# Experts' token lists made inside the experts' stage, in column strips, and causal masks over two tiles

## The reference, cut to what matters

```
# causal layer: 12 heads of width 16, T = 256
att = einsum('bhqd,bhkd->bhqk', q, k) * D ** -0.5
att = where(tril(ones((T, T))), att, -inf)
# experts: n = 8192 tokens, E = 16, capacity = 1024
scores = sigmoid(x @ gate_weight.T)
topk_score, topk_ids = top_k(scores.T, capacity)      # per expert, over the tokens
xg = x[topk_ids]
out = (silu(xg @ Wg) * (xg @ Wu)) @ Wd * topk_score
y = zeros((n, d)).at[topk_ids].add(out)
```

## Time and profile before

| | us |
|---|---|
| median of 3 runs | 5709.36 |
| lowest and highest run | 5707.49, 5717.35 |
| profiled execution, its own time | 5669.09 |
| its span in the profile | 5667.3 |
| TensorE busy in the span | 5117.5 (90%) |
| VectorE busy | 3504.7 (62%) |
| ScalarE busy | 2573.6 (45%) |
| GpSimd busy | 1120.5 (20%) |

### The profile page before, as it was taken

One profiled execution on the slowest core, in us unless ns is written; L12 is line 12 of the kernel. 1 busy time (PEld: TensorE's weight loads), 2 busy tenths in 40 slices (PEclk: granted clock), 3 DMA queues, 4 the chain that ended last, 5 costly groups with the idle time before them and its releaser, 6 DMA issues. The chain is left out here.

```text
span 5667.3 us, 119255 instructions
## 1 busy us (share of the span) xinstructions
PE 5117.5 (90%) x41810; PEld 4014.3 (71%) x41810; DVE 3504.7 (62%) x8939; ACT 2573.6 (45%) x5128; POOL 1120.5 (20%) x1056
## 2 busy tenths in 40 slices
PE   0799999999999999999999999699999822899999
PEld 0578777777778777778777777477777612677777
DVE  6566666666666666666666666577777577222222
ACT  0355555555555555555555555355555500111111
POOL 6111111111111111111111111000000002333343
PEclk9999999999999999999999999899999956999999
DMA  6544444444444444444444444244444200333332
GB/s 104 102 96 93 86 98 94 103 94 95 86 96 96 103 92 95 87 94 97 103 94 95 87 96 95 68 90 92 95 96 92 70 6 6 98 65 82 85 86 40
DMA packets 1283993, 488.96 MB, mean 86 GB/s; under 512 B 1086531, under 2 KB 1270560, under 8 KB 1283872
## 3 DMA queue, kind: packets, MB, share of 16 engines
q1 hardware_dynamic: 1256224, 450.68, 36.5%
q0 software_dynamic: 27648, 36.72, 4.1%
HBM read 162.87 MB, written 60.28 MB: 39 GB/s over the span
## 5 line engine op out<-in xcount | busy, mean ns | idle before, releaser
L754 ACT ACTIVATE pT<-banks 128x384 f32<-128x384 f32 x1920 | 924.9, 491 | 785.4 <-PE banks L524 785.0
L972 DVE TENSOR_REDUCE mx<-banks 128x4 f32<-128x768 f32 x768 | 719.0, 949 | 293.6 <-PE banks L506 293.5
L1155 POOL TENSOR_TENSOR rstd<-ve,half 128x2 f32<-128x2 f32 x288 | 218.8, 760 | 3069.5 <-DVE ve L881 3069.5
L504 PE MATMUL banks<-maskb,eyeb 128*128 128x384 bf16 x1920 | 633.8, 330 | 52.2 <-DMA qkT<-stack 25.3
L506 PE MATMUL banks<-qkT 128*128 128x192 bf16 (+2 forms) x3840 | 634.6, 247 | 0.0
L524 PE MATMUL banks<-qkT 128*128 128x192 bf16 (+2 forms) x3840 | 632.3, 247 | 0.0
L622 PE MATMUL banks<-w,pT 128*128 128x192 f32 x3072 | 554.5, 330 | 0.0
L622 PEld LDWEIGHTS banks<-w,pT 128*128 128x128 f32 x3072 | 492.7, 190 | 42.4 <-issue 21.9
L522 PE MATMUL banks<-mseq,eyeb 128*128 128x384 bf16 x1536 | 501.4, 326 | 10.0 <-DMA qkT<-mrT 5.7
L608 PE MATMUL banks<-nT,w 128*128 128x256 f32 x1920 | 473.3, 383 | 7.2 <-DMA b<-in_b 3.1
L1915 PE MATMUL ps_g<-exp_xT,exp_wg 64*128 64x512 f32 x1152 | 476.0, 594 | 1.0 <-ACT exp_xT L1829 1.0
(11 more groups left out here) (202 smaller groups left out, 8909.9 us busy)
## 6 DMA issues: line engine op xcount, KB each, us to landing
hcur<-hbuf SPq DMA_DIRECT2D x164, 192.0 KB, 2.6
resid<-hbuf SPq DMA_DIRECT2D x160, 192.0 KB, 2.5
amb<-am_d SPq DMA_DIRECT2D x130, 192.0 KB, 3.0
hbuf<-hout SPq DMA_DIRECT2D x128, 192.0 KB, 2.0
exp_wg<-in_ewg SPq DMA_DIRECT2D x16, 768.0 KB
exp_wu<-in_ewu SPq DMA_DIRECT2D x16, 768.0 KB
exp_wd<-in_ewd SPq DMA_DIRECT2D x16, 576.0 KB
xs<-xr SPq DMA_DIRECT2D x32, 272.0 KB, 2.2
```

The source lines that it names most:

```text
L504: nc.tensor.matmul(dst[:, 0:SCOLS], eyeb[:], maskb[:, masks, :], start=True, stop=False)
L754: ph.inc(nc.scalar.activation(pT[s][:, h % NPT, :], bank[s][h % 2][:, 0:SCOLS], ACT.Exp, scale=SCALE), "p", s)
L972: last = nc.vector.tensor_reduce(mx[s][:, :, at].rearrange("p t h -> p h t"), src[:, :, 0:SCOLS].rearrange("p h (t k) -> p h t k", t=T), A ...
```

## The change

`choose` and `experts` become one block, `route`. All weights' loads of the first two experts are issued at its start, behind the inputs of the search. The search, the ranks and the transposes are as before. GpSimd makes no table steps any more; all four are VectorE's. Lists 0 and 1 and the table of list 2 come before the loop; list j of the others is made two experts ahead, inside the loop: its products between `gate_up` and `transposes`, its table's four steps one behind each quarter of `weigh` of the expert before. The 64 products of a list go in turn to four column strips (16 to each), so that the result is four partial lists on 128 partitions; VectorE joins place and group (`read_strips`), a product with a 0/1 matrix adds the four strips (`ids_sum`), VectorE reads the list (`read_ids`), SyncE stores it and loads it back. The list's results share the banks of `ps_y`, so `down` waits until the list is read. In the causal layer the mask product covers the two diagonal tiles only, 256 columns in place of 384, and the other tile starts from what the score product writes.

```diff
+        def pe_mask(ph, dst, mask):
+            part = lambda x: x[:, 0:SCOLS]
+            if ph is not tok:
+                part = lambda x: x[:, 0:SCOLS].rearrange("p (x c) -> p x c", c=P)[:, 0:3:2, :]
+            nc.tensor.matmul(part(dst), eyeb[:], part(mask), start=True, stop=ph is not tok)
...
-            nc.tensor.matmul(dst[:, 0:SCOLS], eyeb[:], maskb[:, masks, :], start=True, stop=False)
+            pe_mask(ph, dst, maskb[:, masks, :])
...
+            def keep_ids(j, u):
+                sp.wait_ge(idi_ok[u], j + 2)
+                dst = ids_d[bass.ds(j * 2 + u, 1), :].rearrange("o (h l) -> (o h) l", l=32)
+                sp.dma_start(dst, ids_i[u][:]).then_inc(ids_st[u], 16)
+
+            def load_ids(j, u):
+                sp.wait_ge(ids_st[u], j * 16 + 17)
+                sp.dma_start(idx[u][:], ids_d[bass.ds(j * 2 + u, 1), :].rearrange("o (p g) -> (o p) g", g=G)
+                             ).then_inc(i_in[u], 16)
             for u in U:
-                load(u, u)
+                weights(u, u)
+            for u in U:
+                keep_ids(0, u)
+                load_ids(0, u)
             with sp.Fori(0, E // 2 - 1) as i:
                 for u in U:
+                    keep_ids(i + 1, u)
                     sp.wait_ge(y_st, (i * 2 + u + 1) * (16 * G))
-                    load(i * 2 + u + 2, u)
+                    load_ids(i + 1, u)
+                    weights(i * 2 + u + 2, u)
...
+            def table_step(j, u, k):
+                grid = [P, NBLK, SEG, 32]
+                lane = iotab[:].unsqueeze(1).unsqueeze(1).to_broadcast(grid)
+                part = lambda w: hlT[:, w, :, bass.ds((j * 2 + u) * SEG, SEG)].unsqueeze(3).to_broadcast(grid)
+                if k == 0:
+                    dve.wait_ge(idp_ok[u], j + 1)
+                    lo = oh_lo[u][:].rearrange("p (c s) w l -> p c s w l", s=SEG)
+                    nc.vector.tensor_tensor(lo[:, :, :, 0, :], lane, part(1), ALU.is_equal).then_inc(oc[u], 1)
...
+            def read_strips(j, u):
+                dve.wait_ge(idp_ok[u], j + 2)
+                nc.vector.tensor_copy(ids_f[u][:], ps_id[u][:, 0:32]).then_inc(if_ok[u], 1)
+                dve.wait_ge(if_ok[u], j + 1)
+                nc.vector.scalar_tensor_tensor(out=ids_s[u][:], in0=ps_id[u][:, 32:64], scalar=float(P),
+                                               in1=ids_f[u][:], op0=ALU.mult, op1=ALU.add).then_inc(strip_ok[u], 1)
+
+            def read_ids(j, u):
+                dve.wait_ge(sum_ok[u], j + 1)
+                dve.wait_ge(ids_st[u], j * 16 + 1)
+                nc.vector.tensor_copy(ids_i[u][:], ps_sum[u]).then_inc(idi_ok[u], 1)
...
+                    hidden(i * 2 + u)
+                    read_strips(i + 1, u)
+                    read_xT(i * 2 + (u + 1), (i + 1, u))
+                    weigh(i * 2 + u, u, i + (1 + u) if u < tables else None)
...
+            def ids(j, u):
+                pe.wait_ge(y_ok, (j * 2 + (u - 2)) * NX + 1 if not isinstance(j, int) or j else 1)
+                pe.wait_ge(oh_ok[u], j + 1)
+                pe.wait_ge(hi_ok[u], j + 1)
+                pe.wait_ge(idi_ok[u], j + 1)
+                for t in range(NTILE):
+                    n = t % 4
+                    last = nc.tensor.matmul(ps_id[u][32 * n:32 * n + 32, :], oh_hi[u][:, t, :],
+                                            oh_lo[u][:, t].rearrange("p w l -> p (w l)"),
+                                            start=(t < 4), stop=(t >= NTILE - 4), tile_position=(0, 32 * n))
+                last.then_inc(idp_ok[u], 1)
+
+            def ids_sum(j, u):
+                pe.wait_ge(strip_ok[u], j + 1)
+                nc.tensor.matmul(ps_sum[u], strip[:], ids_s[u][:], start=True, stop=True).then_inc(sum_ok[u], 1)
...
+                if listed:
+                    pe.wait_ge(idi_ok[u], i + 3)
                 pe.wait_ge(hid_ok, e * NF + (NF + 1))
...
                 gate_up(i, 0)
-                transposes(i, 1)
+                ids(i + 1, 0)
+                transposes(i, 1, (i + 1, 0))
                 down(i, 0)
```

More of the change, by code:

```diff
@@ L204, in build @@
         tower(nc, a, hbuf, am_d, xs, sd, out, B, L)
-        choose(nc, a, sd, ids_d, N, CAP)
-        experts(nc, a, xs, ids_d, out, N, CAP)
+        route(nc, a, xs, sd, ids_d, out, N, CAP)
 def embed(nc, a, hbuf, am_d, B, V, HROWS):
@@ L1530, in choose @@
     NTILE = SEG * NBLK
-    HI = CAP // 32
+    G = CAP // P
+    HALF = 512
+    NHALF = CAP // HALF
+    y_out = out.rearrange("b s d -> (b s) d")
+    U = (0, 1)
     with ExitStack() as ctx:
-        sb = lambda name, shape, dt: ctx.enter_context(nc.sbuf_tensor("sel_" + name, shape, dt))
         sem = Semaphores(nc)
[L1535 to L1565, removed]
@@ new lines, in _, with gather, scatter @@
+            sp.wait_ge(y_st, 16 * G * E)
+        @block.gpsimd
+        def _(pool):
+            def gather(i, u):
+                wait_apart(pool, i_in[u], i * 16 + 16, eye_in, 16)
+                for g in range(G):
+                    pool.indirect_dma_start(xg[u][:, g, :], None, xs,
+                                            bass.IndirectOffsetOnAxis(ap=idx[u][:, g:g + 1], axis=0)
+                                            ).then_inc(g_in[u], 16)
+            def scatter(i, u):
+                if not (isinstance(i, int) and i * 2 + u == 0):
+                    pool.wait_ge(y_st, (i * 2 + u) * (16 * G))
+                for g in range(G):
+                    if g % 2 == 0:
+                        wait_apart(pool, y_ok, (i * 2 + u) * NX + (g // 2 + 2), eye_in, 16)
+                    pool.indirect_dma_start(y_out, bass.IndirectOffsetOnAxis(ap=idx[u][:, g:g + 1], axis=0),
+                                            yb[u][:, g, :], None, compute_op=ALU.add).then_inc(y_st, 16)
+            pool.wait_ge(eye_in, 16)
+            gather(0, 0)
+            gather(0, 1)
+            for u in U:
+                scatter(0, u)
+                gather(1, u)
+            with pool.Fori(1, E // 2 - 1) as i:
+                for u in U:
+                    scatter(i, u)
+                    gather(i + 1, u)
+            for u in U:
+                scatter(E // 2 - 1, u)
@@ L1698, in _ @@
+            for k in range(4):
+                table_step(1, 0, k)
+                if k == 1:
+                    read_strips(0, 1)
+                if k == 3:
+                    read_ids(0, 1)
+            read_xT(0)
+            with dve.Fori(0, E // 2 - 2) as i:
+                pair(i, 2)
+            pair(E // 2 - 2, 1)
+            hidden(E - 2)
+            read_xT(E - 1)
+            weigh(E - 2, 0)
+            hidden(E - 1)
+            weigh(E - 1, 1)
         @block.tensor
@@ L1887, in transposes @@
+            def transposes(i, u, listed=None):
                 e = i * 2 + u
@@ L1889, in transposes @@
                 for k in range(NX):
+                    if k == 2 and listed is not None:
+                        ids_sum(*listed)
                     if k >= 2:
```

349 lines of the change are left out of this document (147 added, 202 removed).

## The result

| | before, us | changed, us |
|---|---|---|
| median | 5708.42 (4 runs, 5701.23 to 5717.35) | 5543.12 (4 runs, 5541.42 to 5553.33) |
| profiled execution, its own time | 5669.1 | 5544.2 |
| its span | 5667.3 | 5542.4 |

The account below looks back on a forecast made before the run. TensorE was taken to bound the causal layer and experts, with VectorE's list making between them. -149 + 29 - 17 = -137 us from a median of 5709.4 gave 5573 us; 8-in-10 range 5530 to 5609.

Parts of the forecast that it names:

- Front, -149: From the first table step to an expert's first transposes: making only the first lists ahead saves 149 us, bounds 144 to 152.
- The hold-up of the first gather: Before the experts: VectorE, still making list 2's table, can hold up GpSimd's gathers; +2 us taken.
- Lists inside the experts, +29: In the experts: 14 lists' products on TensorE at 2.1 us each add 29 us, bounds +10 and +44.
- GpSimd's hold-up: In each expert: VectorE's four table steps may hold the scatter up by at most 7.6 us, hidden by the gathers' room.
- Masks, -17: Causal layer: mask products over two tiles save 0.54 us a turn over 31 full turns, 17 us; bounds 0 and -41.
- The offset of 40.3 us: Whole kernel: the median before lies 40.3 us above the profiled execution, and the change was taken to leave that untouched.
- masks in full: Rival, causal layer: the shorter masks pay all 41 us, giving 5548 us; chance 0.10.
- masks for nothing: Rival, causal layer: the shorter masks pay nothing, giving 5590 us; chance 0.12.
- the list's chain as a wait: Rival, experts: reading strips, sum and list takes twice 1.7 us, down products start 0.9 us late, +13 us, 5586; chance 0.06.
- GpSimd beyond its room: Rival, experts: GpSimd is held up some 15 us instead of 7.6, costing 3 us x 14, 5615 us; chance 0.07.
- the emptied array: Rival, list products: each change of strip empties TensorE's array, 14.5 us a list, 5746 us, slower; chance 0.04.
- The period of 53.4: Sign in the experts: the time from one expert to the next becomes 53.4 us, from 51.27, through about 2 us of list products.

Follow-up runs that it names:

- the jobs: Three sets of follow-up runs, timed apart from the result's: kernel before 5667 to 5669 us, changed kernel 5511.6 us, ratio 0.9724.

## Why the prediction was right, and where it was off

- **Front, -149.** Measured -149.1 in the result's traces and -150.1 in those of the jobs. The single steps err against each other: counted from the first table step, list 0 is read 0.7 us earlier than forecast (15.1, not 15.85), the index load goes out 1.5 us later (18.8, not 17.25), the eight gathers and their landing take 12.6 us in place of 12 and 2. List 0's products took 1.04 us at the granted clock 0.50 (the 1.2 GHz level), not 3.7, hidden in either case.
- **The hold-up of the first gather.** It took 1.88 us, not the 1.02 of the earlier trace rows, beside VectorE's table step: 0.9 us where I took 2. That the front came out within 1 us owes something to luck, since errors of 1 to 2 us cancel.
- **Lists inside the experts, +29.** The step that failed is "the instruction, not the 64 columns, looks like the floor, so strips gain little". 29 ns was right for one strip (29 between starts, 26.1 in the mean); four strips give 9.7. And most of the 29 ns were the 64 columns (27 ns by the rate of the gate and up products), which different strips take at the same time. A list costs 0.62 us on TensorE, and 0.54 on the period. In the traces without the stall the stage's +7.8 us were below my lower bound of +10: it had 0.71 us a list, the way in and out of the strips included, where 0.62 is measured; the shorter wait on VectorE's copy (0.17 us, before 0.43 in this place) pays for the sum product. The Trainium skill (TensorEngine Tiling (Array Packing), Theoretical Speedup) says up to four times for 32 columns; the runs show 2.7 (26.1 against 9.7 ns). The Trainium skill (TensorE: Matmul & The Clock Gate, "Wait — 56ns, not 53.3ns?") says that starts never come closer than about 25 ns; the trace disagrees across strips, 9.7 ns, and in one strip, where they are 29 ns apart, it doesn't test the floor.
- **Down's wait on the list: none.** Room 0.95 us, forecast 0.8.
- **GpSimd's hold-up: at most 7.6 us, hidden.** Measured 5.8, hidden, and it grows no further when the steps are doubled. The Trainium skill (SBUF — State Buffer, "SBUF: two separate sides") describes an exclusive lock of the port pair that VectorE and GpSimd share, held for the whole instruction. The trace agrees: the step of 4723.53 ends at 4725.81, 2.09 us behind the scatter's start at 4723.72; with the scatter's own 1.56 that is 3.65 us, and it took 3.54.
- **Masks, -17.** Measured -15.8 and -16.8 in the traces, -18 in the medians of the masks alone. The mechanism is shown: the wait on the row maxima grew from 0.32 to 0.80 us, as forecast, and fell away when the stack moved.
- **The offset of 40.3 us** between the profiled execution and the median, "nothing in the change touches the difference". The step carried an offset into the forecast that isn't a property of the kernel: in the jobs the kernel before has none (profiled 5665.5, median 5666.4), and the changed kernel has none in the result (profiled 5544.2, median 5543.1). What the result's runs do have is 31.5 us over those of the jobs in the changed kernel (5543.1 against 5511.6), and there the profiled execution has it too. Its span is 37.9 us longer than that of the jobs: 2.9 up to the first table step, 1.3 up to the transposes, 4.0 ahead of the first products and 29.7 from them to the end, where the stall is.
- **The sum.** In the jobs, without the stall, 155.6 us were gained by the medians (159.2 by the spans), of 137 forecast; the terms err by 21 us in the lists and 1 in the front. In the result's runs it was 165 by the medians and 124.9 by the spans. So the median of 5543 came about by errors that cancel: the profiled execution took 5544.2 and not 5532, with 22 us less for the lists and the front and 38 of stall and delay that I didn't foresee (the rest, 4 us, is the difference of the two kernels before); and its median lies 1 us below it, not 40 above. That 5543 is 30 us from the forecast and not more is in part luck. That the kernel gains by the terms named isn't: the gain of 155.6 in the jobs lies within the forecast's range as well (100 to 179). The low end of that range takes 14 us for the lists and not their bound of 10.

The rivals: masks in full and masks for nothing are both out in this kernel (-18); the list's chain as a wait, GpSimd beyond its room and the emptied array didn't happen. The period of 53.4 that I named as a sign did appear, for a wrong reason: about 2 us of stall, not 2 us of products. The duration of the 64 products told them apart at once; the period alone would have confirmed a wrong step.

Open: what the stall is, and with it where the 40 us of the kernel before lie. In the one trace that has it, it begins about 23 us behind the start of gate and up, near the end of a burst of gathers, but the releasers named there are transfers long done. The rows above show that the products ahead of VectorE's pause end at 4753.89 and VectorE goes on only at 4755.58, where it otherwise follows at once. The same bursts pass without a stall in the jobs. The instruction queues moved 71 and 52 packets, as in the jobs, and only one of them in ten stalled experts, so it isn't a reload of code. No run brought it back.

## What to carry over

Price products in column strips by a row of the same shape with the strips side by side; where there is none, keep the low bound in the range. When work on a tightly followed engine gets shorter, look at once at which engine it will wait for next, and move that one's work that isn't needed yet: here that was worth as much as the shorter masks themselves (16 to 23 us against 18 to 27), and more beside them than alone. A sign named in advance should be the duration of the step itself, not a period that other things can also give.

## What the runs showed of the hardware

- 64 products of 64 columns in four column strips: 9.7 ns each at the granted clock 1.00; one strip after another 26.1 ns.
- 128 more products in TensorE's loop body brought 55 more instruction packets and some 2 us of wait a pass; 64 more brought 1 packet and no wait.
- An indirect scatter of 1.56 us takes up to 3.59 us beside a VectorE operation on two tensors.
- One and the same kernel took 5708 us in the result's runs and 5667 to 5669 us in those of the three jobs; the changed one 5543 and 5512.
